# An inverse-square-root helper with one more step, and a handover between two token groups in another order (cross-attention and quantised feed-forward, one core)

## The reference, cut to what matters

```
x = x + xattn(layernorm(x), ctx)          # x: 8 x 1024 x 512, ctx: 8 x 64 x 512
    lat = layernorm(.) * w + b ; c = layernorm(ctx) * w + b
    q = lat @ Wq ; k, v = split(c @ Wkv)  # 16 heads of 64
    attn = softmax(clip(q k^T / 8, -11, 11))
    out = attn v @ Wo + bo
x = x + ffn(layernorm(x))                 # fake-quantised: x by one scale for all of it,
    gate, up = xq @ Wg^T, xq @ Wu^T       # weights by one scale a row
    h = fake_quant(silu(gate) * up)
    out = h @ Wd^T
```

## Time and profile before

| what | value |
|---|---|
| three runs | 1322.95, 1323.09, 1324.69 us, median 1323.09 |
| the profiled execution | 1323.09 us, its span 1321.0 us, so 2.1 us lie outside the span |
| granted TensorE clock, as a share of full speed | 0.999 |
| opening | 0 to 83 us of the span |
| attention loop | 83 to 823 us |
| feed-forward | from 823 us |
| TensorE busy | 97% of the span |
| VectorE busy | 88% |
| ScalarE busy | 60% |

### The profile page before, as it was taken

One profiled execution on the slowest core, in us unless ns is written; L12 is line 12 of the kernel. 1 busy time (PEld: TensorE's weight loads), 2 busy tenths in 40 slices (PEclk: granted clock), 3 DMA queues, 4 the chain that ended last, 5 costly groups with the idle time before them and its releaser, 6 DMA issues.

```text
span 1321.0 us, 20706 instructions
## 1 busy us (share of the span) xinstructions
PE 1283.0 (97%) x7800; PEld 604.6 (46%) x7800; DVE 1157.6 (88%) x2052; ACT 788.5 (60%) x1186; POOL 357.6 (27%) x261
## 2 busy tenths in 40 slices
PE   7999999999999999999999999999999999989998
PEld 4644444544445445445444444444444444434333
DVE  7777988998899899888989858789999999799997
ACT  6688577557757755775675561433343333599760
POOL 3105243134224413422441320000000000056556
PEclk9999999999999999999999999999999999999999
DMA  7276147246345462562462381386756632299996
GB/s 295 80 232 184 49 128 215 73 120 200 101 150 133 116 210 59 151 220 74 127 210 76 117 249 51 127 224 259 248 201 238 260 97 65 107 373 424 427 417 233
DMA packets 179267, 241.74 MB, mean 183 GB/s; under 512 B 121680, under 2 KB 140896, under 8 KB 168160
## 3 DMA queue, kind: packets, MB, share of 16 engines
q1 hardware_dynamic: 179168, 240.43, 55.3%
HBM read 120.86 MB, written 90.57 MB: 160 GB/s over the span
## 4 chain that ended last, share of the span: by engine, by line
PE 64%; DVE 15%; ACT 10%; DMA 4%; issue 3%; SPq 2%; POOL 1%; DVEq 0%; ACTq 0%; POOLq 0%
PE pg L1552 10%; PE pu L1558 10%; PE po L77 7%; PE po L79 7%; PE po L78 7%; PE ring L77 6%; PE ring L78 6%; PE ring L79 6%; ACT hb L1439 5%; DVE w L1519 2%; DMA hb<-hidden 2%; ACT E L452 1%; DMA x<-in_x_dram 1%; PE ring L1039 1%; PE ring L1066 1%
## 5 line engine op out<-in xcount | busy, mean ns | idle before, releaser
L1419 ACT ACTIVATE sg<-pg,gate_scale 128x512 f32<-128x512 f32 x176 | 120.9, 687 | 186.3 <-PE pg L1552 186.3
L77 PE MATMUL ring<-yT,M 128*128 128x512 f16 x512 | 194.1, 379 | 0.0
L79 PE MATMUL ring<-yT,M 128*128 128x512 f16 x512 | 194.0, 379 | 0.0
L78 PE MATMUL ring<-yT,M 128*128 128x512 f16 x512 | 194.0, 379 | 0.0
L1552 PE MATMUL pg<-xqT,w 128*128 128x512 bf16 x704 | 180.7, 379 | 4.1 <-DMA xqT<-xq 2.9
L77 PE MATMUL po<-VW,p 128*128 128x512 f16 x480 | 182.2, 380 | 1.7 <-DVE p L660 1.7
L79 PE MATMUL po<-VW,p 128*128 128x512 f16 x480 | 181.9, 379 | 0.0
L78 PE MATMUL po<-VW,p 128*128 128x512 f16 x480 | 181.9, 379 | 0.0
L1558 PE MATMUL pu<-xqT,w 128*128 128x512 bf16 x704 | 180.7, 379 | 0.0
L395 POOL TENSOR_TENSOR esum<-esum,E 128x512 f32<-128x512 f32 x96 | 130.3, 1358 | 83.9 <-ACT E L456 83.9
L660 DVE TENSOR_TENSOR p<-E,p 128x512 f16<-128x512 f32 x120 | 140.8, 1174 | 9.1 <-ACT p L467 9.0
(11 more groups left out here) (242 smaller groups left out, 2205.1 us busy)
## 6 DMA issues: line engine op xcount, KB each, us to landing
hidden<-hb SPq DMA_DIRECT2D x11, 2816.0 KB, 9.7
hb<-hidden SPq DMA_DIRECT2D x11, 2816.0 KB, 18.5
xa<-x_rows_d SPq DMA_DIRECT2D x28, 1024.0 KB, 6.7
x<-in_x_dram SPq DMA_DIRECT2D x16, 1024.0 KB, 5.6
value_fold<-E SPq DMA_DIRECT2D x64, 256.0 KB, 2.5
VW<-value_fold SPq DMA_DIRECT2D x16, 1024.0 KB, 6.1
x_rows_d<-x SPq DMA_DIRECT2D x16, 1024.0 KB, 4.6
out_dram<-xa SPq DMA_DIRECT2D x11, 1024.0 KB, 12.6
```

Of the source, the lines that this page charges most:

```text
L77: nc.tensor.matmul(out, a_hi, b_hi, start=first, stop=False)
L78: nc.tensor.matmul(out, a_hi, b_lo, start=False, stop=False)
L79: return nc.tensor.matmul(out, a_lo, b_hi, start=False, stop=last)
L1419: nc.scalar.activation(sg[:, n % 4], pg[n % 4][:], ACT.Silu, scale=gate_scale[:, n % FT:n % FT + 1]).then_inc(silus, 1)
```

## The change

It does three things.

1. `rsqrt` takes its first guess in two integer instructions (shift right by one; times -1 plus the constant) in place of one (times -0.5 plus the constant). `RSQRT_OPS` goes from 10 to 11.
2. In the opening, at n = 5, `q_high(0)` (ScalarE) and `q_low(0)` (VectorE) move behind the halving of the value weights' chunk.
3. At the end of stage 0 the normalisation of group 2 is moved. VectorE: `norm_stats(2)` from t = 4 to t = 6; `norm_aggregates(2)` and `norm_rstd(2, 2)` from t = 5 and t = 6 to behind the last `fold_value`; `invert(0)` from ahead of `low_y(2, 0)` and `low_y(2, 1)` to behind them. ScalarE: `high_y(2, 0)` and `high_y(2, 1)` from behind `exp(1, 1)` in stage 1 to the end of stage 0, ahead of `cap(1, 0)`.

```diff
-RSQRT_OPS = 10
+RSQRT_OPS = 11
...
-    done(nc.vector.tensor_scalar(y.bitcast(i32), v.bitcast(i32), -0.5, float(0x5F3759DF), ALU.mult, ALU.add))
+    done(nc.vector.tensor_scalar(y.bitcast(i32), v.bitcast(i32), 1, None, ALU.logical_shift_right))
+    done(nc.vector.tensor_scalar(y.bitcast(i32), y.bitcast(i32), -1.0, float(0x5F3759DF), ALU.mult, ALU.add))
...
             kv_high(0, n)
-            if n == 5:
-                q_high(0)
             if n < 6:
                 weight_high(1, n - 2)
             if n < 4:
                 square(1, wq32[:, n], n)
+            if n == 5:
+                q_high(0)
...
                 exp(s, t)
-                if s == 1 and t == 1:
-                    high_y(2, 0)
-                    high_y(2, 1)
...
             if s == 0:
+                high_y(2, 0)
+                high_y(2, 1)
                 continue
...
             if n == 5:
                 scale_by_rows(WQ, misc[:, 0:P], 2, 4)
-                q_low(0)
             if n < 6:
                 weight_low(1, n - 2)
...
+            if n == 5:
+                q_low(0)
...
-                    if t == 4:
+                    if t == 6:
                         norm_stats(2)
-                    if t == 5:
-                        norm_aggregates(2)
-                    if t == 6:
-                        norm_rstd(2, 2)
                     continue
...
             if s == 0:
+                norm_aggregates(2)
+                norm_rstd(2, 2)
                 norm_rows(2, 0)
                 norm_rows(2, 1)
-                invert(0)
                 low_y(2, 0)
                 low_y(2, 1)
+                invert(0)
                 continue
```

## The result

The changed kernel takes 1331.97 us (median of four executions, 1331.32 to 1332.78) against 1323.67 us for the kernel before, run beside it on the same chip (four, 1322.95 to 1324.69): ratio 1.0062, 95% interval 1.0048 to 1.0076. It is slower, as forecast, but by 8.3 us in place of 4.4, and outside the range of 1324.0 to 1329.6. Its profiled execution took 1328.48 us (span 1326.4, clock 0.997), only 5.4 us above the profiled one of before. So two questions follow: are the 5.4 us of the two traces what was forecast, and where do the other 3 us come from? (Clock in this document is the mean granted TensorE clock, as a share of full speed.)

The account below looks back on a forecast made before the run. TensorE was busy for 97% of the span, VectorE for 88%, so TensorE's waits counted. Terms 0.6 + 2.2 + 0.6 + 0.6 + 0.45 = 4.4 us on 1323.1 gave 1327.5 us; own range 1326.2 to 1328.8, wider 1324.0 to 1329.6.

Parts of the forecast that it names:

- Opening: Up to turn_q(4): one more rsqrt instruction, +0.20 us, and q_low(0) starting later, +0.41 us; +0.6 us together.
- Handover: Group 0 to group 1: ScalarE idles ahead of high_y(2, 0), so high(0, 0) and TensorE's resumption come later, +2.2 us.
- isn't what decides: In the handover: invert(0) behind low_y makes the division ready at 119.9 us, earlier than ScalarE wants it.
- Stages: rsqrt calls for groups 3 to 15: six stages at 0.1 us, +0.6, and three calls at full price, +0.6.
- Feed-forward start: Two rsqrt calls in VectorE work that TensorE and then ScalarE wait for: 0.25 + 0.20 = +0.45 us.
- Contended again: Rival: GpSimd's adding meets the new chain, one to two instructions of 1.1 us; 1328.6 us or more, chance 0.06.
- The base: Time of the kernel before, taken from its profiled execution, 1323.09 us, also the median; the terms were added to 1323.1.
- every call pays: Rival: the sum of exponentials is just in time in all stages, 2.6 us for 1.2; 1328.9 us, chance 0.11.
- The handover gains: Rival: the faster chain and earlier values remove TensorE's waits of 3.3 us; -1.1 us, 1322.0 us, chance 0.08.

Follow-up runs that it names:

- order_q_only: The kernel before with only q_high(0) and q_low(0) moved behind the chunk of the value weights: 1324.77 us, ratio 1.0003 to before.
- act_as_before: The changed kernel with ScalarE's high_y(2, 0) and high_y(2, 1) back behind exp(1, 1): 1333.95 us, ratio 1.0065 to the kernel before.
- pad18: The kernel before with 18 one-column memsets added on VectorE in the opening: 1326.32 us, ratio 1.0013 to before.
- after_pad18: The changed kernel with 18 one-column memsets added on VectorE in the opening: 1328.92 us, ratio 1.0026 to the kernel before.
- after_pad40: The changed kernel with 40 one-column memsets added on VectorE in the opening: 1332.06 us, ratio 1.0050 to the kernel before.
- pad18_gpsimd: The kernel before with 18 one-column memsets added on GpSimd at its start: 1324.99 us, ratio 1.0006 to before.
- handover_only: The kernel before with only the new order at the end of stage 0 (part three): 1328.69 us, ratio 1.0029 to before.
- norm_late_only: The kernel before with only VectorE's norm_stats, norm_aggregates and norm_rstd of group 2 moved later: 1324.85 us, ratio 1.0005 to before.
- after_filled: The changed kernel with matmuls whose result nobody reads put into five of TensorE's waits: 1330.80 us, ratio 1.0044 to the kernel before.
- helper_twice: The kernel before with rsqrt of 12 instructions, the new first guess and a multiplication by 1.0: 1332.86 us, ratio 1.0066 to before.

## Why the prediction was too low

- **Opening, +0.6.** Right. `turn_q(4)` starts 0.78 us later; the order of `q_low` is 0.40 of it (0.41 forecast), as order_q_only shows alone. The executions of unchanged openings spread by 0.5 us (49.17 and 49.66 in kernels that don't touch it), so the rest isn't told from noise; the 0.40 is, since it is a distance within one trace. By the time order_q_only can't be told from no change.
- **Handover, +2.2.** Right: 2.87 us at TensorE's resumption, less the 0.78 of the opening, is 2.09. Steps of 0.2 us, idleness of ScalarE of 4.91 ("about 5"), `high(0, 0)` at 123.11 ("about 123"), TensorE at 140.63 (140.5): all as written. Measured alone 2.6 us. One sentence failed: that `invert` behind `low_y` "isn't what decides". In the change it isn't, but in act_as_before, with ScalarE's idleness down to 1.66 us, the division behind it is what `high(0, 0)` waits for.
- **Stages, 0.6 + 0.6.** Right in size, 1.37 us against 1.2, and partly by luck. The last two stages took 0.36 of it, with the wait at the stage of 738 us 0.46 in place of 0.28, where three calls at full price were to give 0.6. The other 1.0 came from all eleven stages before, some 0.1 each, where only every other one was to pay. The wait of 0.1 us of TensorE at `denominators` that was to show it isn't there; only the weight load's grew, from 0.21 to 0.41 us. Where in a stage the 0.1 lies was not looked for.
- **Feed-forward start, +0.45.** Right: 0.43.
- **"Contended again".** The prediction let the added instruction cost up to 1.1 us more wherever GpSimd is adding. No trace tests this: the eleventh instruction never fell beside an addition, and took 0.17 us (0.19 on sixty columns) in all 18 calls.
- Up to the first feed-forward matmul the sum was 4.4 and the trace has 4.67 (838.53 less 833.86).
- **After it: nothing was forecast, and 0.9 us came.** Here a step of the prediction failed: the calls of `rsqrt` were priced by their duration alone. An added instruction also moves the loading of all later ones, and one of these loads now falls beside the last transpose ahead of the third group. This is shown by pad18, after_pad18, after_pad40 and pad18_gpsimd.
- **The base, 1323.1 us.** "The profiled execution took 1323.09, which is also the median" rested on three executions and took the clock of 0.999 as given. The 77 executions of the kernel before that were timed beside the experiments have a mean of 1324.64 us and a mean clock of 0.9968: 1.5 us lie there. What they have and the profiled one lacks wasn't traced. In order_q_only, handover_only and norm_late_only, whose third group waits as long as that of before, it is a low stretch behind this wait (447.7 to 448.1 us to the end in place of 446.5).
- **The clock of the changed kernel, the largest error.** Its 16 executions have a mean clock of 0.9936. At 0.73 us for each 0.001 that is 2.4 us more than before, and no term had it: the step that failed is the sum, which priced each wait as the time that it lasts. What the runs showed in its place is 1.7 us of work lost behind a wait, at two places in one trace of the changed kernel where the other trace lost none. That the lower clock is a cause and no companion rests on this pair of traces of one kernel, with 1.69 and 1.7 us in two segments; after_filled, which gave back 1.9 of the mean, agrees but isn't clear of the noise. Why a wait of 1.5 us is followed by the lower level in one execution and not in the other stays open.

Together: 1324.6 + 4.8 + 2.4 = 1331.8, the mean of the changed kernel's executions (1331.82); by the way the fit is made this must add up. The forecast's 1327.5 lacks 1.5 of base, 0.4 of the terms and 2.4 of clock. The traces split the same 4.3 us otherwise: 1.5 of base, 1.0 of the terms (5.4 between the two spans, 0.9 of it the DMA wait) and 1.8 of further low stretches. The fit counts the harmless stretch at 120 us, which the kernel before doesn't have, as clock; the split of the traces rests on one execution of each. Both have the same three sources, and their sizes are known to half a microsecond or so.

Of the rivals, "every call pays" was nearest in time (1328.9) and at best half right in cause: its 13 calls were to cost 2.6 us and cost 1.4 to 1.6, though each of them paid something. "The handover gains" is refuted by `high(0, 0)` at 123.11 where it asked for 118; "contended again" by eleven steps of 0.2 us.

## What to carry to other kernels

Price a new wait of a TensorE that is otherwise full twice: as its length, and as the chance of 1.7 us of lost work behind it, if TensorE is the bound there; and give the base of a sum the mean clock of many executions, not that of the profiled one. When a term can't be found in the work, look at the instruction queues in the DMA view: code that does nothing, put elsewhere, moves the loads. When a reordering on two engines costs time, put each half back by itself before blaming either: here neither paid alone.

## What the runs showed of the hardware

- VectorE's instructions arrive in packets of some 8 KB, on a queue that carries those of other engines as well (queue 14: 38 packets, 0.31 MB in the whole span). Eighteen more memsets on VectorE moved the packet near the third feed-forward group from 11.0 us after to 1.6 us ahead of its first matmul, and the transpose beside it took 3.5 us in place of 2.5.
- After waits of TensorE of 1.1 to 3.5 us (at 50, 120, 140, 810, 840 and 880 us) the granted clock fell to the lower level, a mean of 0.83 to 0.86 over 10 us, in some executions and not in others. Where TensorE was the bound, this lengthened a segment by 1.7 us; in the changed handover, where ScalarE is, it cost nothing.
- A float instruction of VectorE on four columns beside an addition of GpSimd took 1.27 us with a single tensor input (the multiplication by 1.0 in helper_twice), as long as those with two, where it takes 0.17 in the other groups' calls; the integer instruction just ahead of it met no addition:

```profile
110.29 0.17 DVE L68 TENSOR_SCALAR rs<-rs 128x4 int32<-128x4 int32 x1
110.50 1.27 DVE L69 TENSOR_SCALAR rs<-rs 128x4 f32<-128x4 f32 x1
111.81 1.19 DVE L71 TENSOR_TENSOR rt<-rv,rs 128x4 f32<-128x4 f32 x1
```
